# Two minimum operations per group moved from VectorE to GpSimd, with GpSimd's steps reordered around them

## The reference, cut to what matters

```
q_proj = _elu1(jnp.einsum('bhnd,hdf->bhnf', q, proj_matrix))   # elu1(x) = where(x > 0, x + 1, exp(x))
k_proj = _elu1(jnp.einsum('bhnd,hdf->bhnf', k, proj_matrix))
kv = jnp.einsum('bhnf,bhnd->bhfd', k_proj, v)
attn = jnp.einsum('bhnf,bhfd->bhnd', q_proj, kv)
z = 1.0 / (jnp.einsum('bhnf,bhf->bhn', q_proj, k_sum) + 1e-08)
x = _layernorm(x + (attn * z) @ w_out + b_out)
expert_id = jnp.argmax(x @ wr + br, axis=-1)
x = _layernorm(x + expert_mlp(x, expert_id))      # gelu(x w1 + b1) w2 + b2 of the token's expert
```

## Time and profile before

| | before |
|---|---|
| median of 3 runs | 273.26 us (273.2 to 273.49) |
| profiled execution, its own time | 275.39 us |
| its span, first to last instruction | 273.7 us |
| mean granted TensorE clock | 0.883 |
| busy PE / DVE / ACT / POOL | 76% / 69% / 56% / 42% of the span |
| one query step, s = 4 to 7 | 11.2 us |
| query stage, from the first query chunk to the start of step 8 | about 76 to 158 us |

### The profile page before, as it was taken

One profiled execution on the slowest core, in us unless ns is written; L12 is line 12 of the kernel. 1 busy time (PEld: TensorE's weight loads), 2 busy tenths in 40 slices (PEclk: granted clock), 3 DMA queues, 4 the chain that ended last, 5 costly groups with the idle time before them and its releaser, 6 DMA issues.

```text
span 273.7 us, 6269 instructions
## 1 busy us (share of the span) xinstructions
PE 207.9 (76%) x1749; PEld 163.6 (60%) x1749; DVE 188.3 (69%) x665; ACT 153.2 (56%) x414; POOL 114.2 (42%) x153
## 2 busy tenths in 40 slices
PE   0789999999787768747775055879399999999900
PEld 0477777777543453433522033789299999999800
DVE  0446666666657999999999967447577777777730
ACT  1357777777577556674665204466337767667500
POOL 8000000000400306484655807256647777777770
PEclk9979999999999968968599557679869999999985
DMA  4011110097000101111111147236436877767000
GB/s 129 2 38 41 38 39 25 24 289 203 8 0 2 40 1 58 45 56 40 40 58 57 41 113 219 83 114 174 136 93 192 216 226 203 223 178 211 21 15 0
DMA packets 25377, 25.25 MB, mean 92 GB/s; under 512 B 3529, under 2 KB 18158, under 8 KB 25344
## 3 DMA queue, kind: packets, MB, share of 16 engines
q1 hardware_dynamic: 23072, 20.59, 26.7%
q0 software_dynamic: 2272, 4.27, 4.5%
HBM read 20.04 MB, written 5.26 MB: 92 GB/s over the span
## 4 chain that ended last, share of the span: by engine, by line
POOL 29%; issue 27%; PE 25%; DVE 8%; ACT 3%; DVEq 2%; SPq 1%; DMA 1%; POOLq 0%; ACTq 0%
PE pair L288 13%; POOL sorted_rows L458 10%; POOL out_dram L481 7%; PE bank L553 6%; POOL rstd L477 5%; POOL rstd L443 3%; POOL xg L432 3%; DVE y L1058 2%; DVEq L280 2%; PE bank L528 1%; PE pair L516 1%; DVE qfeat L865 1%; DMA bout_col<-in_L_attn_b_out_dram 1%; PE pair L649 1%; POOL vals L437 1%
## 5 line engine op out<-in xcount | busy, mean ns | idle before, releaser
L787 ACT ACTIVATE qfeat<-pair,b_cols 128x128 f32<-128x128 f32 x156 | 44.6, 368 | 24.5 <-PE pair L649 24.4
L481 POOL DMA_INDIRECT out_dram<-y,xs x39 | 39.3, 1009 | 20.6 <-DVE y L1058 14.5
L649 PE MATMUL pair<-xsT,w_slot 128*128 128x128 f32 x312 | 44.8, 290 | 0.0
L649 PEld LDWEIGHTS pair<-xsT,w_slot 128*128 128x128 f32 x312 | 41.3, 206 | 0.1
L288 PE MATMUL pair<-wkv_part,xT_all 128*128 128x256 f32 x192 | 38.2, 338 | 0.7 <-ACT vals L712 0.5
L432 POOL TENSOR_TENSOR xg<-xg,bout_sb 128x512 f32<-128x512 f32 x8 | 10.3, 1282 | 63.7 <-DMA xg<-in_L_attn_x_dram 63.5
L458 POOL DMA_INDIRECT sorted_rows<-x,dest x32 | 31.9, 998 | 9.0 <-issue 9.0
L288 PEld LDWEIGHTS pair<-wkv_part,xT_all 128*128 128x128 f32 x192 | 30.0, 196 | 6.3 <-ACT xT_all L698 4.9
L288 PE MATMUL pair<-xT_all,wq_part 128*128 128x512 f32 x96 | 31.6, 459 | 1.5 <-DVE qfeat L865 1.3
L443 POOL TENSOR_TENSOR rstd<-var_eps,minus_half 128x4 f32<-128x4 f32 x8 | 8.4, 1053 | 53.7 <-DVE var_eps L906 53.7
L659 PE MATMUL bank<-w_sb,qfeat 128*128 x152 | 21.7, 290 | 4.7 <-DVE yx L1040 4.7
(11 more groups left out here) (148 smaller groups left out, 409.8 us busy)
## 6 DMA issues: line engine op xcount, KB each, us to landing
w_slot<-in_L_ffn_w_dram SPq DMA_DIRECT2D x39, 256.0 KB
xs<-sorted_rows SPq DMA_DIRECT2D x39, 66.0 KB, 3.3
xr<-in_L_attn_x_dram SPq DMA_DIRECT2D x8, 256.0 KB, 2.9
xg<-in_L_attn_x_dram SPq DMA_DIRECT2D x8, 256.0 KB, 2.8
out_dram<-y,xs POOLq DMA_INDIRECT x39
sorted_rows<-pad_rows SPq DMA_DIRECT2D x8, 66.0 KB, 1.7
b_sb<-in_L_ffn_b_dram SPq DMA_DIRECT2D x1, 512.0 KB, 14.2
sorted_rows<-x,dest POOLq DMA_INDIRECT x32, 2.4
```

The lines of the kernel that those rows point to most:

```text
L481: g_.indirect_dma_start(out=out_rows, out_offset=bass.IndirectOffsetOnAxis(ap=xs[:, t % XS, D:D + 1].bitcast(I32), axis=0), in_=y[:, t % N ...
L649: last = mm(h_bank[t % 2][:, k * P:(k + 1) * P], w1_slot[:, t % WB, k * P:(k + 1) * P], xsT[:, t % 2, :], start=True, stop=True)
L787: a_.activation(hT[:, t % 2, k * P:(k + 1) * P], h_bank[t % 2][:, k * P:(k + 1) * P], ACT.Gelu, bias=b1_cols[:, bass.ds(c_at[t] + k, 1)]). ...
```

## The change

The minimum of chunks 1 and 3 is taken off VectorE and given to GpSimd, in a new function `at_most_one`. GpSimd's own step is put in another order: the minimum of chunk 1 and `residual_base` come first, then the group's token numbers and `rstd`, then the minimum of chunk 3, and the scatters last.

```diff
+            def at_most_one(g, k):
+                n = g * C + k
+                pool.wait_ge(q_exp, n + 1)
+                g_.tensor_scalar(qexp[:, n % QB, :], qexp[:, n % QB, :], 1.0, None, ALU.min).then_inc(q_min, 1)
+
             def group_step(s):
+                if s < G:
+                    at_most_one(s, 1)
+                    residual_base(s)
                 if 0 <= s - 2 < G:
                     token_numbers(s - 2)
                     inverse_deviation(s - 2)
+                if s < G:
+                    at_most_one(s, 3)
                 if 0 <= s - 3 < G:
                     scatter(s - 3, range(GT))
-                if s < G:
-                    residual_base(s)
...
             def q_features(g, k):
                 n = g * C + k
-                dve.wait_ge(q_exp, n + 1)
                 reach(dve, attn_pre, g - 1)
                 if k in BY_RELU:
+                    dve.wait_ge(q_exp, n + 1)
                     v.scalar_tensor_tensor(...).then_inc(q_done, 1)
                 else:
-                    v.tensor_scalar(qexp[:, n % QB, :], qexp[:, n % QB, :], 1.0, None, ALU.min).then_inc(q_min, 1)
                     dve.wait_ge(q_min, g * (C - len(BY_RELU)) + k // 2 + 1)
                     v.scalar_tensor_tensor(...).then_inc(q_done, 1)
```

## The result

The changed kernel took 301.93 us (median of 4 runs, 300.04 to 303.25) against 273.38 us for the kernel before (median of 4): a ratio of 1.1007, 95% interval 1.0956 to 1.1058. The forecast was 288.0 with a range of 284.5 to 293.0, so the time lies 8.9 us above the range. The sign and the wait for the refill came as forecast, the size did not: 28.5 us lost where 14.6 were expected. The price of GpSimd's minimum was 1.49 us and not 0.61.

The account below looks back on a forecast made before the run. VectorE's list was taken to bound the query stage at 11.21 us a step. Steps of 13.83 us make chunk 3 of step 7 15.6 late, less 1.33 at the tables: 288.0 us for the median, range 284.5 to 293.

Parts of the forecast that it names:

- The sign: Whole kernel: slower with chance 0.94, the same 0.01, faster 0.05.
- the wait for the refill: GpSimd's bias, moved ahead of rstd, waits for the DMA into xg, landing 2.7 us after its issue.
- What bounds the kernel, and what is removed: Query stage: VectorE's list bounds the 11.21 us step; it loses 2.3 us a step, and the tables a 1.33 us stall.
- The move and its wait: Middle step, chunk 1 to rstd: refill wait and bias ahead of rstd make 6.46 us of 3.50, adding 2.96 a step.
- The price of a minimum: GpSimd's minimum on 128x512: 0.61 us, from the selects; range 0.53 to 1.27.
- the term m: Time of one GpSimd minimum, taken as 0.61 us; it enters the middle step twice, 12.61 + 2m = 13.83 us.
- the minimum on GpSimd is dear: Rival: GpSimd's minimum costs 0.95 to 1.3 us, giving 291.6 us at 0.95 and 295 at 1.27; chance 0.12.
- The number of minima on the path: Query stage: ten to eleven minima lie on the path, so each 0.1 us of price costs 1.05 us.
- The rival on the other side: Middle steps: the refill is not waited for, the loop is 10.87 us and the kernel takes 269.8 us; chance 0.05.

Follow-up runs that it names:

- later-bias kernel: Kernel before, with GpSimd's bias addition delayed until VectorE has combined chunk 1 of the next step: 267.58 us against 275.65, ratio 0.9751; again 268.10 against 273.58.
- p2_two_op_price: Kernel before with extra one- and two-operation GpSimd instructions on unread data, in idle time ahead of the key stage: query-stage stretch 80.71 us, 124.7 behind it.

## Why the prediction was right, and where it was wrong

*What bounds the kernel, and what is removed.* Right. The stall of VectorE's minimum, of `scaled` and of `t_row` is the bias's doing: `t_row` fell from 1.50 to 0.16 us in the changed kernel and in the later-bias kernel, and the four long minima to 0.42 or 0.43 in the latter. Undoing all six stalls, 8.2 us, gained 7.6 and 7.3 us of the stretch.

*The move and its wait.* Right, and the largest term: 2.96 us a step and 17.8 in six steps were forecast; taking the wait away gave 16.9 us with the dear minimum and 17.2 with the cheap one. Step for step, between the changed kernel and the one with a third buffer, it is 2.6 to 3.0 us.

*The price of a minimum.* This is the step that failed: the term m in the sum of the middle step. I bounded it by writing alone (0.53) and the two-input addition (1.27), as if no one-input form could be dearer than a two-input one, and took 0.61 by the selects. It is 1.49, outside both bounds; and the range's upper end went by 0.95 only. The price runs show a select of 512 numbers at 0.60 and a min-max at 0.61, so the value was that of other instructions. The rival "the minimum on GpSimd is dear" had the mechanism, with 0.12, but ended at 295 us with its bound of 1.27.

*The number of minima on the path.* I counted ten to eleven and called steps 0 and 1 nearly free. By the kernel with the cheap form it was about 13 of 16 (11.4 us for 0.88 each): 10.2 from chunk 1 of step 2 on, as counted, and 2.7 of the five before. In steps 0 and 1 of the changed kernel VectorE waited 1.39, 1.62, 1.36 and 1.62 us for the four.

*The sum of the miss.* 301.93 - 288.0 = 13.9 us. The price of the minimum accounts for 11.4: 9.2 at the 1.05 us for each 0.1 that I had counted, 2.1 by the minima that I had not. The stretch with the assumed price came out 0.3 above the sum (15.0 against 14.7). The start of the query stage was 0.66 later and the tile stage 0.44 shorter in the profiled executions, 0.2 together. The last 2.0 are in the step from the profiled execution to the median: I took off the 2.1 us by which the kernel before's own profiled execution stood above its median (275.39 against 273.26), and the changed kernel's stood 0.1 above its own (302.02 against 301.93).

*The rival on the other side* had its chance: with a third buffer and the assumed price the stretch is 2.2 us shorter than before, and the time is the same within its interval, where the rival had 3.4 us less. It needed two conditions, no wait for the refill and the cheap minimum, and the changed kernel had neither.

## What to carry to other kernels

Before an instruction is moved ahead of another on an in-order engine, look at what it waits for, not only at what it costs: the bias took 1.7 us of GpSimd's time and its DMA, issued by a semaphore of the same step, 2.7 more, on the path of everything behind it. A buffer count that is enough for the old order may be one too few for the new. And an engine's idle time of 3.3 us a step is worth nothing to work that stands elsewhere in its list; a price that no row shows wants a measurement of that very form, since its nearest relative was off by a factor of 2.4.

## What the runs showed that was not expected

- On GpSimd a tensor_scalar of 128x512 float32 with one operation took 1.49 us for max, add and mult and 1.48 for min in place; min with another output took 1.83 and 1.93. Min took 0.84 us for 256 numbers and 0.52 for 128. Min then max or mult then add took 0.61 us; min then max took 0.39 for 256 and 0.28 for 128. Min then min took 1.92. A copy took 0.79 us, a select 0.60, a subtraction of two tensors 1.28.
- The stretch of the query stage is alike over chips to 0.5 us for the order of before (80.63, 80.71, 80.17) and to 0.1 for the changed kernel (107.01, 106.88), while what follows took 114.7 to 116.0 us on some chips and 122.2 to 126.6 on two others. TensorE is busy 91.4 us of this part in `p2_two_op_price` and 88.7 in the kernel before, at a granted clock of 0.86 and 0.85. So most of the 9.2 us that it is longer there are idle time, and 4.5 of them are waits for the DMA of the sorted rows, of which the kernel before shows none. Why these come later isn't known.
